# Attention with experts: the gated columns of a unit are split into halves in SBUF and turned by transposing SyncE transfers, and its second product takes five matmuls

## The reference

```python
xn = _layernorm(x)
q, k, v = (split_heads(xn @ W + b) for W, b in ((Wq, bq), (Wk, bk), (Wv, bv)))
scores = jnp.where(causal, jnp.einsum('bhqd,bhkd->bhqk', q, k) / 4.0, -jnp.inf)
attn = jnp.einsum('bhqk,bhkd->bhqd', softmax(scores), v) @ Wo + bo

topk_w, topk_idx = jax.lax.top_k(softmax(xn @ gate_w.T), 4)
combine = zeros.at[rows, topk_idx].add(topk_w / topk_w.sum())
a = silu(xn @ w_gate[e]) * (xn @ w_up[e]) * combine[:, e]
y = sum over e of a @ w_down[e]
y = y + (silu(xn @ sw_gate) * (xn @ sw_up)) @ sw_down
return x + attn + y
```

## Time and profile before

| | |
|---|---|
| Runs | 1176.25, 1179.19, 1183.70 us, median 1179.19 |
| Span of the profiled execution | 1354.9 us; its own time beside the span is not recorded |
| TensorE matmuls busy | 1007.9 us, 74% |
| VectorE | 866.0 us, 64% |
| ScalarE | 654.5 us, 48% |
| GpSimd | 579.2 us, 43% |
| Transfers | 126.41 MB, mean 93 GB/s |

### The profile page before, as it was taken

One profiled execution on the slowest core, in us unless ns is written; L12 is line 12 of the kernel. 1 busy time (PEld: TensorE's weight loads), 2 busy tenths in 40 slices (PEclk: granted clock), 3 DMA queues, 4 the chain that ended last, 5 costly groups with the idle time before them and its releaser, 6 DMA issues.

```text
span 1354.9 us, 26394 instructions
## 1 busy us (share of the span) xinstructions
PE 1007.9 (74%) x8634; PEld 525.7 (39%) x8634; DVE 866.0 (64%) x1784; ACT 654.5 (48%) x1219; POOL 579.2 (43%) x531
## 2 busy tenths in 40 slices
PE   2788121010399999898998989998988989899885
PEld 1555010000144444444544444454444445444433
DVE  6888831000288887777777676676767676677553
ACT  3778100000154545565566666556666665566341
POOL 6333177776200000454366666435656553464100
PEclk9888555555599999899999999999989999899888
DMA  6899450010113131443545355354535353444702
GB/s 175 270 297 283 125 180 1 1 34 1 43 56 105 54 104 48 88 85 75 89 80 112 63 111 95 66 89 78 111 57 112 56 112 64 88 71 73 134 17 31
DMA packets 99484, 126.41 MB, mean 93 GB/s; under 512 B 24873, under 2 KB 83514, under 8 KB 98834
## 3 DMA queue, kind: packets, MB, share of 16 engines
q0 software_dynamic: 41632, 60.79, 25.0%
q1 hardware_dynamic: 57730, 63.99, 16.1%
HBM read 71.63 MB, written 57.80 MB: 96 GB/s over the span
## 4 chain that ended last, share of the span: by engine, by line
PE 53%; DVE 10%; another core or an unknown queue 10%; issue 9%; ACT 2%; SPq 1%; DMA 1%; POOL 0%; ACTq 0%; DVEq 0%
PE gup L1221 12%; PE pvp L1144 10%; PE outs L1248 9%; DVE part L1314 6%; PE smp L1100 6%; PE turn L1233 4%; PE stp L1125 4%; PE outs L1151 3%; PE turn L1191 3%; PE smp L1083 1%; ACT probs L1484 1%; DVE hf L1371 1%; DVE sg L1366 1%; DMA Qs<-nm 1%
## 5 line engine op out<-in xcount | busy, mean ns | idle before, releaser
L1484 ACT ACTIVATE probs<-stp 128x1024 f32<-128x1024 f32 (+1 forms) x320 | 300.4, 939 | 424.4 <-remote 205.2
L1314 DVE TENSOR_REDUCE part<-smp 128x2 f32<-128x256 f32 (+2 forms) x372 | 345.9, 951 | 140.0 <-remote 72.5
L942 POOL DMA_INDIRECT XG<-xrow_d,slots x144 | 146.8, 1019 | 247.0 <-DMA out<-Y 201.7
L1221 PE MATMUL gup<-gu_w,XC 128*128 (+1 forms) x1152 | 212.8, 321 | 32.7 <-issue 21.8
L1100 PE MATMUL smp<-Ks,Qs 48*128 48x128 f16 (+2 forms) x744 | 112.5, 341 | 103.7 <-DVE part L1314 52.4
L1248 PE MATMUL outs<-dn_w,h 88*128 (+1 forms) x1248 | 183.6, 280 | 0.1
L949 POOL DMA_INDIRECT out<-Y,slots x72 | 117.1, 1626 | 139.1 <-ACT Y L1517 107.8
L1144 PE MATMUL pvp<-probs,Vs 128*32 128x512 f32 (+3 forms) x1536 | 168.8, 512 | 0.8 <-DVE probs L1413 0.7
L949 POOL DMA_INDIRECT acc_d<-Y,slots x72 | 114.7, 1594 | 123.7 <-ACT Y L1517 104.6
L1221 PEld LDWEIGHTS gup<-gu_w,XC 128*128 128x128 f16 x1152 | 107.2, 99 | 96.1 <-issue 43.5
L931 POOL DMA_INDIRECT slot_d<-entry,slot_i x128 | 124.3, 971 | 41.6 <-issue 41.6
(11 more groups left out here) (170 smaller groups left out, 1109.6 us busy)
## 6 DMA issues: line engine op xcount, KB each, us to landing
rb<-rsum_d SPq DMA_DIRECT2D x60, 128.0 KB
Ks<-k_d SPq DMA_DIRECT2D x96, 64.0 KB
Qs<-q_d SPq DMA_DIRECT2D x96, 64.0 KB
v_d<-V SPq DMA_DIRECT2D x8, 544.0 KB, 4.6
Vs<-v_d SPq DMA_DIRECT2D x16, 272.0 KB, 3.0
acc_d<-YA SPq DMA_DIRECT2D x1, 4224.0 KB
X<-L_attn_x POOLq DMA_DIRECT2D x8, 512.0 KB, 5.0
xrow_d<-XR SPq DMA_DIRECT2D x8, 512.0 KB, 5.0
```

The lines of the kernel that those rows point to most:

```text
L942: pool.indirect_dma_start(XG[:, q].rearrange("p a c t -> p (a c t)"), None, s.xrow_d, bass.IndirectOffsetOnAxis(ap=slots[:, r, 0:1], axis= ...
L1221: last = pe.matmul(gup[:, 0:2 * I], columns[:, a, h], weights_of(s.gu_w, e, b, h, slice(0, 2 * I)), start=n == 0, stop=n == 5)
L1314: last = dve.tensor_reduce(part[:, g % 2, k0 // CH, :, j, t], banks[:, :, col:col + w], AX.X, ALU.max)
L1484: act.activation(to, of, ACT.Exp, scale=float(DK) ** -0.5 / QS ** 2).then_inc(exp_done, 1)
```

## The change

The gated columns stay where they are made, 128 rows by 176 columns. ScalarE writes their high part to SBUF and VectorE the low part, into a float16 tile `HX` of 128 x 384: columns 0 to 127 hold the first 128 high columns, 256 to 383 the first 128 low ones, and the middle block holds the last 48 high columns and, 64 further on, the last 48 low ones (the rest is zero). One transposing SyncE transfer turns the three blocks into `HT`. The second product becomes five matmuls: three over 128 rows, one over 112 rows (both parts of the last 48 columns against the high weights, which are stored twice) and one over 48 rows. Some of the float32 scratch goes: `sg` is merged with `th`, `hf` has two buffers instead of three, and two of the three `HX` lie in the tile of the routing logits.

The two parts are made in the slots one and two behind the first half; the transfer is in SyncE's program two slots behind it, after that slot's other issues listed above. LAG is 3, and the planner's cost of a second half 600. The down weights are laid out for it: `dn_w` has 128 partitions and four blocks, and `prepare` loads each down matrix by three transfers instead of one, after clearing the second block.

```diff
-        dn_w = sb("dn_w", [IP, EW, 2, 2, D], F16)
+        dn_w = sb("dn_w", [P, EW, 4, D], F16)
...
-                pool.dma_start(dn[:, n], d.rearrange("(c p) n -> p c n", p=IP)).then_inc(gu_in[n], 16)
+                pool.dma_start(dn[:, n, 0], d[0:P]).then_inc(gu_in[n], 16)
+                for r in (0, P // 2):
+                    pool.dma_start(dn[r:r + IT, n, 1], d[P:P + IT]).then_inc(gu_in[n], 16)
...
-        FB = 3
+        FB, XB, TB = 2, 3, 3
+        HW = 3 * P
...
+        hx2 = sb("hx2", [P, HW], F16)
+        lg16 = s.logits[:, :, :].rearrange("p t e -> p (t e)").bitcast(F16)
+        HX = [lg16[:, 0:HW], lg16[:, HW:2 * HW], hx2[:, :]]
+        HT = sb("HT", [P, TB, 3, P], F16)
...
+        def gated_turned(v):
+            return ht_in[v % TB], 16 * (v // TB + 1)
...
-            cost = [(880 if shared_of(v) is not None else 1200, 980)[h] for h, v in halves]
+            cost = [(880 if shared_of(v) is not None else 1200, 600)[h] for h, v in halves]
...
-        LAG, SPARE = 2, 4
+        LAG, SPARE = 3, 4
...
+        first_slot = {v: g * SLOTS + n for (g, n), v in FIRST.items()}
+        HIGH = {divmod(k + 1, SLOTS): v for v, k in first_slot.items()}
+        LOW = {divmod(k + 2, SLOTS): v for v, k in first_slot.items()}
...
+            def turn_gated(v):
+                sp.wait_ge(hl_done, v + 1)
+                if v >= TB:
+                    sp.wait_ge(y_done, v - TB + 1)
+                sp.dma_start_transpose(HT[:, v % TB], HX[v % XB]).then_inc(ht_in[v % TB], 16)
...
             def turn_rows(r):
...
-                pe.wait_ge(hl_done, turned_h[0])
...
-            def turn_h(v):
-                pe.wait_ge(hf_done, v + 1)
-                if v:
-                    pe.wait_ge(hl_done, v)
-                if turned_rows[0]:
-                    pe.wait_ge(xc_done, turned_rows[0])
-                for c in range(2):
-                    last = pe.transpose(hp[:, c * P:(c + 1) * P], hf[:, v % FB, c * IP:(c + 1) * IP], s.ident[:, :])
...
             def down(v, projected):
...
-                pe.wait_ge(hl_done, v + 1)
+                pe.wait_ge(*gated_turned(v))
...
-                for c in range(2):
-                    for a, b in PASSES:
-                        last = pe.matmul(yp, h16[:, v % 2, a, c], weights_of(s.dn_w, e, b, c, slice(0, D)),
-                                         start=begin and n == 0, stop=end and n == 5)
-                        n += 1
+                for n, (c, rows, b) in enumerate(((0, P, 0), (0, P, 1), (2, P, 0), (1, IZ, 2), (1, IT, 3))):
+                    last = pe.matmul(yp, HT[0:rows, v % TB, c], weights_of(s.dn_w, rows, e, b, slice(0, D)),
+                                     start=begin and n == 0, stop=end and n == 4)
...
                     def second_half():
-                        turn_h(z)
-                        if z:
-                            down(z - 1, projected)
-                        return outs_before(z)
+                        down(z, projected)
+                        return outs_before(z + 1)
...
             def low_part(v):
                 dve.wait_ge(hh_done, v + 1)
-                dve.tensor_tensor(h16[:, v % 2, 1].rearrange("i c t -> i (c t)"), hp,
-                                  h16[:, v % 2, 0].rearrange("i c t -> i (c t)"), ALU.subtract).then_inc(hl_done, 1)
+                x, h = HX[v % XB], hf[:, v % FB]
+                dve.tensor_tensor(x[:, 2 * P:3 * P], h[:, 0:P], x[:, 0:P], ALU.subtract)
+                dve.tensor_tensor(x[:, P + P // 2:P + IZ], h[:, P:I], x[:, P:I], ALU.subtract).then_inc(hl_done, 1)
...
             def high_part(v):
-                act.wait_ge(hT_done, v + 1)
-                if v >= 2:
-                    act.wait_ge(y_done, v - 1)
-                act.activation(h16[:, v % 2, 0].rearrange("i c t -> i (c t)"), hp, ACT.Copy).then_inc(hh_done, 1)
+                act.wait_ge(hf_done, v + 1)
+                if v < XB:
+                    act.wait_ge(hx_clear, XB)
+                else:
+                    act.wait_ge(*gated_turned(v - XB))
+                act.activation(HX[v % XB][:, 0:I], hf[:, v % FB], ACT.Copy).then_inc(hh_done, 1)
```

More of the change, by code:

```diff
@@ L43, in token_mixer_with_experts @@
     HC = D // P
-    IP = I // 2
+    IT = I - P
+    IZ = P // 2 + IT
     TT = T // P
@@ L57, in token_mixer_with_experts @@
     VW = 4 * (DK + 1)
-    assert D == 256 and N % CH == 0 and I % 2 == 0 and DK == 16
+    assert D == 256 and N % CH == 0 and 0 < IT <= P // 2 and DK == 16
     nc.disable_value_cache = True
@@ L345, in expert_parts @@
             return ([one(s.gu_w[:, e, a]).rearrange("p c (a i) -> p c a i", a=2) for a in range(2)],
-                    [one(s.dn_w[:, e, a]) for a in range(2)])
+                    [one(s.dn_w[:, e, a::2]) for a in range(2)])
         @block.scalar
@@ L877, in spread_units @@
             return first, second
-        LAG, SPARE = 2, 4
+        LAG, SPARE = 3, 4
         FIRST, SECOND = spread_units()
         second_slot = {v: g * SLOTS + n for (g, n), v in SECOND.items()}
+        first_slot = {v: g * SLOTS + n for (g, n), v in FIRST.items()}
+        HIGH = {divmod(k + 1, SLOTS): v for v, k in first_slot.items()}
+        LOW = {divmod(k + 2, SLOTS): v for v, k in first_slot.items()}
+        assert all(second_slot[v] >= first_slot[v] + 3 for v in range(NV))
         def half_after(b, h):
             last = (b + 1) * HG * SLOTS + PROJECT_FROM + h * KT + KT - 2
-            return max(v - 1 - SU for v in range(SU + 1, SU + UT + 1) if second_slot[v] <= last)
+            return max(v - SU for v in range(SU, SU + UT) if second_slot[v] <= last)
         HALF_AFTER = {half_after(b, h): (b, h) for b in range(B - 1) for h in range(2)}
         assert len(HALF_AFTER) == 2 * (B - 1)
-        assert second_slot[NV - KT // 2 * SH] < (NG - 1) * SLOTS + LAST_FROM
+        assert second_slot[NV - KT // 2 * SH - 1] < (NG - 1) * SLOTS + LAST_FROM
         def adds_before(r):
@@ L914, in attention_and_experts @@
         xp_done = sem("xp_done"); xc_done = sem("xc_done"); gu_done = sem("gu_done"); th_done = sem("th_done")
-        sg_done = sem("sg_done"); hf_done = sem("hf_done"); hT_done = sem("hT_done"); hh_done = sem("hh_done"); hl_done = sem("hl_done")
+        sg_done = sem("sg_done"); hf_done = sem("hf_done"); hh_done = sem("hh_done"); hl_done = sem("hl_done")
+        ht_in = [sem(f"ht_in{i}") for i in range(TB)]; hx_clear = sem("hx_clear")
         y_done = sem("y_done"); yo_done = sem("yo_done"); added = [sem("added0"), sem("added1")]; merged = sem("merged"); cleared = sem("cleared"); masked = sem("masked")
@@ L924, in _ @@
             pool.memset(sel[:, :], 0.0).then_inc(a_const, 1)
+            for x in HX:
+                pool.memset(x[:, P:2 * P], 0.0).then_inc(hx_clear, 1)
             pool.wait_ge(a_const, 3)
@@ L1037, in after_second @@
             def after_second(v):
-                if 0 < v <= SU and (v - 1) % SH == SH - 1:
-                    t = (v - 1) // SH
+                if v < SU and v % SH == SH - 1:
+                    t = v // SH
                     store_shared(t)
@@ L1220, in gate_up @@
                     for h in range(HC):
-                        last = pe.matmul(gup[:, 0:2 * I], columns[:, a, h], weights_of(s.gu_w, e, b, h, slice(0, 2 * I)),
+                        last = pe.matmul(gup[:, 0:2 * I], columns[:, a, h], weights_of(s.gu_w, P, e, b, h, slice(0, 2 * I)),
                                          start=n == 0, stop=n == 5)
@@ L1295, in _ @@
             values(NG - 1, NST - 1)
-            down(NV - 1, projected)
             pe.wait_ge(ot_done, QC * (NG - 1))
-            for i, over in enumerate(((exp_done, SLOTS * NG), None, (hf_done, NV), (hl_done, NV))):
+            for i, over in enumerate(((exp_done, SLOTS * NG), None, (hf_done, NV), (xc_done, UT))):
                 if over:
@@ L1365, in silu_times_up @@
                 dve.wait_ge(th_done, v + 1)
-                dve.scalar_tensor_tensor(out=sg[:, :], in0=th[:, :], scalar=1.0, in1=gup[:, 0:I],
+                dve.scalar_tensor_tensor(out=th[:, :], in0=th[:, :], scalar=1.0, in1=gup[:, 0:I],
                                          op0=ALU.add, op1=ALU.mult).then_inc(sg_done, 1)
@@ L1503, in second_half @@
             def second_half(v):
-                high_part(v)
-                if v and shared_of(v - 1) is None:
-                    routed_out(v - 1 - SU)
+                if shared_of(v) is None:
+                    routed_out(v - SU)
             def routed_out(r):
@@ L1524, in _ @@
                     exps(g, n)
+                    if (g, n) in HIGH:
+                        high_part(HIGH[g, n])
                     if a is not None:
```

43 lines of the change are left out of this document (20 added, 23 removed).

## The result

The changed kernel takes 1238.95 us (median of four runs, 1233.46 to 1241.82), the kernel before in the same runs 1181.45 us: a ratio of 1.0489, 95% interval [1.0434, 1.0544]. It is slower by 57.5 us. The forecast was 1174 us.

What follows compares the result with a forecast made beforehand. TensorE was taken to bound the stage, with VectorE close behind. Of 104 us saved, 52 are kept: -52 + 45 (late transfers) + 2 (before the stage) = -5 us, so 1179 - 5 = 1174 us, range 1120 to 1245.

Steps and rivals of the forecast that it cites:

- What bounds the kernel: Attention-and-experts stage: TensorE, busy 853 of 935 us, sets the pace until VectorE is what it waits for.
- Part 1: TensorE in the stage: transposes gone 60 us, sixth matmul 19, idle time before transposes 25; 104 us together.
- Part 2: How much of the 104 us VectorE lets through: 52 us kept, bounds 35 to 71; two subtractions 0.46 us.
- 131 units keep 0.21 us: Units directly following another unit's slot keep 0.21 us, the other 77 keep 0.46 us: 63 us remain.
- keep nothing, because the pair of engines takes turns over one score bank: Those 131 units keep nothing, only the other 77 units keep 0.46 us: 35 us remain.
- Part 3: Transposing transfers late in SyncE's order: 0.6 us issue, 2.0 us landing; 45 us lost, ends 13 and about 190.
- 25 late units: Units late for the transfer: seven at slot 3, five at slot 0, eight at slot 7, five first ones.
- Part 4: Before the stage: three transfers per down matrix make loads land later, 2 us, between 0 and 12.
- B: Transposing transfer becomes the pace once issue and landing exceed about 4 us, waits in every group: 1255 us; chance 0.15.
- C: Landing takes 3.0 us, VectorE lets only 35 us through, 25 late units cost 70 us: 1216 us; chance 0.18.
- A: Quick transfers, 0.42 us issue and 1.0 us landing, VectorE lets 71 us through: 1121 us; chance 0.30.
- What would show it: Signs: L1233 gone, some 25 transfer waits of about 2 us, reduction well above 60 us, projection groups shorter, others nearly unchanged.

Runs made afterwards that it cites:

- e1_none: Changed kernel without its 208 transposing transfers, turned tile holding zeros, second product waiting for the low part: 1140.64 us, ratio 0.9647 to the kernel before.
- e6_before_five: Kernel before with five instead of six matmuls in the second product, nothing else changed: 1176.49 us, ratio 0.9952.
- e2_copy: Changed kernel with a plain SyncE copy of the same 96 KB in place of the transposing transfer: 1207.11 us, ratio 1.0207 to the kernel before.

## Why the prediction was wrong, point by point

**What bounds the kernel.** Right. TensorE set the pace and VectorE stood close behind; e1_none and e6_before_five show both.

**Part 1, 104 us of TensorE.** Right in the sum, with some luck in its terms: 72 us busy where 79 were forecast, and 32 us of idle time where 25 were. The 19 us of the sixth matmul cannot be found by themselves: the second product's matmuls are busy 180.9 us before and 178.7 us in e1_none.

**Part 2, 52 us kept.** Too high by 14 us: e1_none gives 38, inside the bounds of 35 to 71 and at their lower end. The two subtractions take 0.28 and 0.20 us and overlap (0.20 and 0.12 us on the chain), 0.40 us together where 0.46 was taken:

```profile
L1384 DVE TENSOR_TENSOR logits<-hf,logits 128x128 f16<-128x128 f32 x132 | 37.2, 282 | 4.0 <-ACT logits L1505 4.0
L1385 DVE TENSOR_TENSOR logits<-hf,logits 128x48 f16<-128x48 f32 x132 | 26.4, 200 | 0.0
```

So the size of VectorE's work was not the error. The step that failed here is the middle taken between "131 units keep 0.21 us" (63) and "keep nothing, because the pair of engines takes turns over one score bank" (35). The runs put it near the second. That the score bank is the reason fits the 44 us on the reduction; it was not tried by itself.

**Part 3, 45 us of late transfers.** This is the step that failed and turned the sign: 98 us. Its mechanism was right in the main, its size was not. Counting the exponentials that had begun by the end of each wait gives its slot: of the 91.5 us, 4.5 are in the first group, 44.1 at slot 3 (13 waits), 9.9 at slots 0 and 1, 9.4 at slot 7, 6.6 elsewhere, and 17.0 is the collision with the 4 MB. The forecast had 5, 24, 6 and 10. The first group and slot 7 came out near their price, but not as reasoned: at slot 7 there were five waits of 1.9 us, not eight of 1.3, so fewer and longer waits cancel there, which is luck. What was mis-sized:

- The issue, 1.18 us instead of 0.6, and the landing, 2.5 us behind the issue's end instead of 2.0: from issue to landing 3.7 us instead of 2.6. VectorE: DVE Perf Modes in the Trainium skill, section "The three transpose paths", gives 1309 ns for a block of 128 x 128, an estimate of 3.9 us for three; the trace agrees with that sum, though e2_copy shows that not the turning but the issue is what a transposing transfer costs more. By the forecast's own arithmetic 1.1 us on 25 late units and 0.6 us on two transfers ahead in seven groups would have been 28 + 8 = 36 us more, 81 in all.
- At slot 3 the seven groups named (1 to 4 and 10 to 12) did wait, and groups 6, 8 and 15 too; in the first three a second unit waited behind the first.
- The collision with GpSimd's 4 MB was in no part of the sum. The row that pointed there was the 4 KB landing of 7.10 us, which was read as a bound of one landing. In that trace it was issued at 1266.18 us, 6 us behind the first of the 4 MB:

```profile
1259.98 3.50 POOL L979 DMA_DIRECT2D out<-acc_d  x4 [2.70 <-DMA acc_d<-Y,slots]
```

- ScalarE's high part, which waits for the transfer three units back, was called hidden. In four units it was not; a late transfer so delays the one three units on, and before the second wait at slot 3 of group 3 the chain goes this way. ScalarE's waits, total, times, longest:

```profile
ACT hx L1505 <- DMA HT<-hx: 6.6, 2, 3.8
ACT logits L1505 <- DMA HT<-logits: 4.9, 2, 3.7
```

- What a stop costs beyond its length. TensorE's busy time is 26.5 us higher than in e1_none for the same instructions, at a granted clock of 0.93 instead of 0.97 over the stretch. The sum had no such term. Against it, other waits shrink: that on the reduction is 45.4 us, 15 less than in e1_none, and those on VectorE's products and on the maxima are 5 less together. That is why 91.5 us of waits and 26.5 us of slower work come to 98 and not 118.

With the measured terms the forecast's sum is -38 + 98 + 0 = +60 us. That it meets the +57.5 us is no test, since both terms are taken from the one kernel e1_none. Of the 65 us between the forecast's -5 and this +60, 53 are part 3 and 14 part 2; part 4 takes 2 back.

**Part 4, before the stage.** 2 us were taken, and nothing was seen: in the first 200 us TensorE does 111.1 us of work before and 111.8 after, and the loop begins at the same time.

**The rivals.** B came nearest (1255 us): the transfers on the chain take 2.3 to 4.6 us but for the collision, with a median of 3.7, just short of its deciding point of about 4 us, and its sign of "beyond 100 us in all" was almost met with 91.5. But there is no wait in groups 5, 9 and 13, where it had one in every group. Its price for the issue, 1.4 us, was nearer than the forecast's. C had the kept 35 us right and a landing of 3.0 us; it counted no longer issue and ended 23 us short. A fell.

**What would show it.** L1233 is gone. The waits lie at slots 0, 3 and 7, 33 instead of 25 and 2.8 us each instead of 2. The reduction's share of the chain is 7.2% of 1035 us, 75 us, so above 60. That groups without projections keep their length while the others get shorter did not come true. With the waits in them, the groups of the changed kernel take from 58.5 to 73.4 us; in e1_none, without these waits, the nine without projections that can be timed are 2.1 us shorter on average than before and the six with them 2.8 us (the planner has spread the units anew, so single groups differ for that too). That VectorE takes back the gain just where no projection runs is not what the groups show.

## What to carry to other kernels

A transfer put in place of engine work is priced by its queue: issue time, everything ahead of it in program order, and the largest transfer that can be under way then, since the engine that waits for it does nothing else until it lands. Walk its queue at the group's turn, where the urgent transfer stands behind bulk loads that no one needs yet; moving those, adding a unit of lead and holding back the 4 MB turned +57 us into -29 us here. And of TensorE time removed beside an engine that is nearly as busy, little came through here: the lower bound held, not the middle.

## What the runs showed of the hardware

A transposing transfer of 96 KB within SBUF holds SyncE 1.18 us, a plain copy of the same bytes 0.47 us; both land some 2.5 us later. Beside 4 MB of GpSimd transfers at 200 GB/s the same transfer took 21.7 us from issue to landing, and 4.7 us with these held back. In a stop of about 12 us the granted clock was 0.50, which is 1.2 GHz, and 0.67 from 2 to 6 us after it; TensorE's six `gate_up` matmuls took 1.88 us then, and 1.04 us three microseconds later. After the stop of 7.1 us in the changed kernel they took 1.76 us.
